# Cross attention's row maxima: one PSUM bank per softmax instead of two banks per group of heads

## The reference, cut to what matters

```
logits_1 = einsum('bhtd,bhsd->bhts', q1, k1) * SCALING
logits_2 = einsum('bhtd,bhsd->bhts', q2, k2) * SCALING
a1 = softmax(logits_1);  a2 = softmax(logits_2)
attn_output = einsum('bhts,bhsd->bhtd', a1 - lam * a2, v)
```

## Time and profile before

| | us |
|---|---|
| median of three runs | 2215.46 |
| the profiled execution | 2225.81 |
| its span, from the first to the last instruction | 2224.0 |
| of it self attention, about | 60 to 800 |
| of it cross attention in steady work, about | 880 to 1700 |
| of it experts and finish, about | 1780 to 2224 |
| VectorE busy over the span | 1303.0 (59%) |
| TensorE matmuls busy over the span | 1711.4 (77%) |

### The profile page before, as it was taken

The page is one execution under the profiler, slowest core; times in us unless marked ns, Lnnn a source line. Parts: engine busy times, 40 slices in busy tenths (PEclk is TensorE's granted clock), DMA queues, the critical chain, the costliest instruction groups (busy, mean ns, idle before and its releaser), DMA issues. The chain is left out here.

```text
span 2224.0 us, 46491 instructions
## 1 busy us (share of the span) xinstructions
PE 1711.4 (77%) x14688; PEld 1214.7 (55%) x14688; DVE 1303.0 (59%) x3032; ACT 1075.7 (48%) x1670; POOL 1236.8 (56%) x1287
## 2 busy tenths in 40 slices
PE   1489999999999845888888888888886359999900
PEld 1356666666666523555555555555553248888800
DVE  2366767676676624777777777777776212222258
ACT  0266666666666523666666666656655112222200
POOL 1566767676676311166666666666665725555423
PEclk9699999999999976988999999989989579999955
DMA  5566666767677426654554545555550035555445
GB/s 197 125 138 158 153 163 147 171 149 171 158 153 168 100 72 106 124 109 98 106 102 101 101 101 102 99 96 103 99 87 25 14 99 124 129 127 126 96 128 179
DMA packets 288971, 267.15 MB, mean 120 GB/s; under 512 B 78962, under 2 KB 273364, under 8 KB 278640
## 3 DMA queue, kind: packets, MB, share of 16 engines
q1 hardware_dynamic: 257648, 244.57, 48.6%
q0 software_dynamic: 22528, 13.03, 3.9%
q10 hardware_dynamic: 8704, 8.39, 1.1%
HBM read 170.57 MB, written 94.30 MB: 119 GB/s over the span
## 5 line engine op out<-in xcount | busy, mean ns | idle before, releaser
L1592 POOL DMA_INDIRECT slot_table<-cross_tok_i,cross_slot_i x384 | 382.6, 996 | 144.6 <-issue 109.3
L598 DVE TENSOR_REDUCE self_nmax<-self_p_mx 128x2 f32<-128x512 f32 x512 | 329.4, 687 | 214.2 <-PE self_p_mx L340 213.8
L1423 DVE TENSOR_REDUCE cross_nmax<-cross_p_mx 128x8 f32<-128x960 f32 x256 | 295.0, 1152 | 210.8 <-PE cross_p_mx L1053 160.0
L510 ACT ACTIVATE self_probs<-self_p_sc 128x1024 f32<-128x1024 f32 x256 | 261.3, 1021 | 95.2 <-PE self_p_sc L328 93.0
L1279 ACT ACTIVATE cross_probs<-cross_p_sc 120x1024 f32<-120x1024 f32 x256 | 261.3, 1021 | 86.0 <-PE cross_p_sc L1037 55.4
L340 PE MATMUL self_p_mx<-self_k_stack,self_q_stack 96*128 96x256 bf16 x1024 | 160.5, 278 | 64.5 <-DMA self_k_stack<-self_k_parts 61.3
L1069 PE MATMUL cross_p_pv<-cross_probs,cross_v_aug 120*32 120x256 f32 x2048 | 176.8, 418 | 9.9 <-ACT cross_probs L1279 6.1
L1053 PE MATMUL cross_p_mx<-cross_k_stack,cross_q_stack 48*128 48x120 bf16 x2048 | 104.5, 225 | 100.4 <-DVE cross_nmax L1423 63.5
L328 PE MATMUL self_p_sc<-self_q_stack,self_k_stack 99*128 99x256 bf16 x1024 | 157.3, 276 | 13.3 <-ACT self_probs L510 12.8
L1956 POOL DMA_INDIRECT expert_sums<-ffn_ye,ffn_idx_add x64 | 92.5, 1445 | 122.0 <-DMA expert_sums<-ffn_ye,ffn_idx_add 53.4
L1037 PE MATMUL cross_p_sc<-cross_q_stack,cross_k_stack 51*128 51x256 bf16 x1024 | 105.8, 287 | 56.5 <-ACT cross_probs L1279 46.7
(11 more groups left out here) (180 smaller groups left out, 3767.6 us busy)
## 6 DMA issues: line engine op xcount, KB each, us to landing
self_q_stack<-self_q_parts SPq DMA_DIRECT2D x64, 256.0 KB, 5.9
cross_q_stack<-cross_q_parts SPq DMA_DIRECT2D x128, 128.0 KB
ffn_w<-in_ffn_w SPq DMA_DIRECT2D x64, 256.0 KB
self_q_parts<-self_parts SPq DMA_DIRECT2D x32, 384.0 KB, 2.8
self_k_parts<-self_parts SPq DMA_DIRECT2D x32, 384.0 KB, 3.8
self_k_stack<-self_k_parts SPq DMA_DIRECT2D x32, 384.0 KB, 8.0
cross_q_parts<-cross_parts SPq DMA_DIRECT2D x64, 192.0 KB
expert_sums<-zero_rows SPq DMA_DIRECT2D x8, 1024.0 KB, 10.2
```

The lines of the kernel that those rows point to most:

```text
L510: act.activation(probs[:, g % 4, :], p_sc[:, :, :].rearrange("p b n -> p (b n)"), ACT.Exp, scale=SCALE).then_inc(s_exp, 1)
L598: dve.tensor_reduce(nmax[:, M.slot, :, m], p_mx[:, m % 2, :].rearrange("p (c k) -> p c k", c=TC), AX_X, ALU.max, negate=True).then_inc(s_r ...
L1423: dve.tensor_reduce(nmax[:, M.slot, :, :, 2 * m:2 * m + 2].rearrange("p c e h -> p e h c"), p_mx[:, :, 0:4 * KEYS].rearrange("p e (x k) -> ...
L1592: pool.indirect_dma_start(out=route[:, :], out_offset=bass.IndirectOffsetOnAxis(ap=slot_i[:, Q.slot, tc, k:k + 1], axis=0), in_=tok_i[:, Q ...
```

## The change

Each group of row maxima is cut into its two softmaxes. TensorE issues the four matmuls of e = 0 and then the four of e = 1, instead of alternating. Before each four it waits until that bank has been reduced in the group before, and after each four it raises `s_mx`. VectorE waits for each bank and reduces it with an instruction of its own (128 x 480 elements to 4 maxima a partition), and each raises `s_red`. So the counts of both semaphores double, to two a group; the one other wait on `s_red`, ahead of the split of the maxima into bf16 parts, counts double too. No memory is added and nothing else is moved.

```diff
-                if m or past(M.n, 1):
-                    pe.wait_ge(s_red, NGR * M.n + m)
-                for hh in range(2):
-                    h = 2 * m + hh
-                    for c in range(TC):
-                        for e in range(E):
+                for e in range(E):
+                    if m or past(M.n, 1):
+                        pe.wait_ge(s_red, E * (NGR * M.n + m) - (E - 1) + e)
+                    for hh in range(2):
+                        h = 2 * m + hh
+                        for c in range(TC):
                             r, q_at = e * HALF, h * T + c * P
                             mm = pe.matmul(p_mx[:, e, (2 * hh + c) * KEYS:(2 * hh + c + 1) * KEYS],
                                            q_stack[r:r + RK, M.slot, q_at:q_at + P],
                                            k_stack[r:r + RK, M.slot, h * KEYS:(h + 1) * KEYS], start=True, stop=True)
-                mm.then_inc(s_mx, 1)
+                    mm.then_inc(s_mx, 1)
...
             def reduce(M, m):
-                dve.wait_ge(s_mx, NGR * M.n + m + 1)
-                if m == 0 and past(M.n, 3):
-                    dve.wait_ge(s_nm, 3 * (M.n - 2))
-                dve.tensor_reduce(nmax[:, M.slot, :, :, 2 * m:2 * m + 2].rearrange("p c e h -> p e h c"),
-                                  p_mx[:, :, 0:4 * KEYS].rearrange("p e (x k) -> p e x k", k=KEYS), AX_X,
-                                  ALU.max, negate=True).then_inc(s_red, 1)
+                for e in range(E):
+                    dve.wait_ge(s_mx, E * (NGR * M.n + m) + e + 1)
+                    if m == 0 and e == 0 and past(M.n, 3):
+                        dve.wait_ge(s_nm, 3 * (M.n - 2))
+                    dve.tensor_reduce(nmax[:, M.slot, :, e, 2 * m:2 * m + 2].rearrange("p c h -> p h c"),
+                                      p_mx[:, e, 0:4 * KEYS].rearrange("p (h c k) -> p h c k", c=TC, k=KEYS), AX_X,
+                                      ALU.max, negate=True).then_inc(s_red, 1)
...
-                    dve.wait_ge(s_red, NGR * (M.n + 1))
+                    dve.wait_ge(s_red, E * NGR * (M.n + 1))
```

## The result

The changed kernel takes 2223.6 us (median of 8 runs), the kernel before took 2215.9 beside it (8 runs): a ratio of 1.0034 [1.0020, 1.0048], so 7.7 us slower. Forecast were 2233 and a range of 2210 to 2256: the sign was right and the size was twice too large. The profiled execution took 2223.86 us, with a span of 2222.1.

What follows compares the result with a forecast made beforehand. Bound: a loop through several engines, with VectorE and TensorE leading in turn. VectorE's 0.30 plus TensorE's 0.35, less 0.04, gave 0.61 us a turn, +18 us over 31 turns: 2215.5 to 2233.5, predicted 2233, range 2210 to 2256.

Steps and rivals of the forecast that it cites:

- VectorE, +0.08 a group, 0.30 a turn: Two reductions of 480 take 1.24 us against 1.152 for one; on the path at m=0 to 3, 0.30 a turn.
- TensorE, +0.15 at m=5 and m=7, 0.35 a turn: Products in softmax order start more slowly, +0.15 us a group on the path at m=5 and m=7; 0.35 with the clock.
- seven steps of which only the one at the seam is free: Eight TensorE products: six of seven steps between starts cost 0.051 us each, 0.31 between first and last start.
- if eight products still take 0.38: Named sign of error: TensorE's eight products of a group lasting 0.38 us as before, where 0.52 was expected.
- m=7 as the way to m=0: TensorE's path runs from L1341 over scores, m=7 and value products to m=0, so m=7's +0.15 us counts.
- the landing 1.96 us behind the modelled end: Before m=0, VectorE's wait was read as products landing later than modelled: 1204.07 against a modelled end of 1202.11.
- The waits added: One more wait on TensorE and one on VectorE; VectorE's costs nothing, TensorE's no more than VectorE's 0.08 us already counted.
- The stretch in which VectorE leads: From m=0 to the end of m=3 VectorE works almost without a gap, so its added time there lengthens the turn.
- Early bank at m=0: Rival: first bank landing at least 0.5 us earlier ends VectorE's reductions sooner at m=0; 2207 to 2211 us, chance 0.13.
- No change: Rival: TensorE's extra 0.15 and half of VectorE's fall into waits; 2216 to 2220 us, chance 0.17.
- The clock: Rival: longer product trains shift TensorE's granted clock either way; 2266 us, or 2205 to 2215; chance 0.12.
- Weight loads laid bare: Rival: each TensorE product runs behind its weight load, +0.97 us a group at m=5 and m=7; 2285 us, chance 0.03.

Runs made afterwards that it cites:

- E1: Kernel before with only VectorE's reduction split in two per group, products in the old order and one signal for both banks: 2219.3 us, 1.0024.
- E8: Kernel before, unchanged, run again for a second profile: 2214.0 us.
- E7: Kernel before with each VectorE reduction cut into four of 240 elements, one signal a group: 2282.4 us, 1.0313.
- E14: Changed kernel with the router's two MAX8 and slots moved behind the reduction of m=4 of the next step: 2171.1 us, 0.9810 of the kernel before.
- E2: Kernel before with only TensorE's order changed, four products of e=0 then four of e=1, waits and signals kept: 2214.7 us, 1.0003.
- E5: Kernel before with VectorE's reduction split only for m=0 to 3: 2216.6 us, 1.0020.
- E10: Kernel before with VectorE's reduction split for every m except m=2: 2214.5 us, 1.0003.
- E11: Kernel before with the router's two MAX8 and slots moved behind the reduction of m=4 of the next step: 2168.7 us, 0.9802.
- E4: Changed kernel with TensorE also waiting for the first softmax's products before issuing the second's: 2303.4 us, 1.0414 of the kernel before.
- E9: Kernel before with VectorE's reduction split only for m=2: 2272.3 us, 1.0265.
- E13: Kernel before with VectorE's reduction split only for m=2 and m=5: 2260.5 us, 1.0205.

## Why the prediction was right in sign and wrong in size

*VectorE, +0.08 a group, 0.30 a turn.* The size of the term was right: 1.22 a pair, 1.24 forecast. E1, which holds this term alone, cost 6.0 us, 9 forecast. Where it lands was only partly right. That its 0.30 a turn comes so near the measured total is luck: 0.09 + 0.32 + 0.06 less the 0.18 that 4>5 and 5>6 give back is 0.29, and the forecast knew neither the step at m=2 nor what is given back. m=0 is not on the path: in E8 the L1443 behind it starts at 1230.59 (above) and ends at 1231.88, just behind GpSimd's L1637, which runs to 1231.72, and takes 1.29 where it takes 0.29 elsewhere. What its reduction adds is lost in that.

```profile
1230.08 1.64 POOL L1637 TENSOR_TENSOR cross_parts<-cross_qk_rest,cross_parts 128x752 bf16<-128x752 f32 x1
```

The distance 0>1 is 4.21 to 4.24 in every kernel of the table but the first profile. m=1 pays 0.09, m=3 0.06, and m=2 pays 0.32, four times its reduction. The price at m=2 has a step in it (E7), and two thirds of the 0.33 sit in the end of L1444 (0.08 + 0.14), the last 0.1 behind the MAX8. GpSimd's chain behind the statistics keeps its own pace. In the change and in E8, the two mask sums together and then the first alone:

```profile
1188.31 0.19 POOL L1655 TENSOR_TENSOR cross_shift<-cross_neg_mean,cross_rstd 128x2 f32<-128x2 f32 x1
1188.46 0.68 POOL L1662 TENSOR_TENSOR cross_mask_sum<-cross_mask_sum,cross_mask 128x64 bf16<-128x64 bf16 x2
...
1188.46 0.30 POOL L1662 TENSOR_TENSOR cross_mask_sum<-cross_mask_sum,cross_mask 128x64 bf16<-128x64 bf16 x1
```

```profile
1238.98 0.20 POOL L1654 TENSOR_TENSOR cross_shift<-cross_neg_mean,cross_rstd 128x2 f32<-128x2 f32 x1
1239.13 0.78 POOL L1661 TENSOR_TENSOR cross_mask_sum<-cross_mask_sum,cross_mask 128x64 bf16<-128x64 bf16 x2
...
1239.13 0.39 POOL L1661 TENSOR_TENSOR cross_mask_sum<-cross_mask_sum,cross_mask 128x64 bf16<-128x64 bf16 x1
```

The mask sums start 2.01 after the statistics in both (1188.46 - 1186.45, 1239.13 - 1237.12). L1443 used to start 0.06 ahead of the first, and took its own 0.29, while GpSimd's took 0.39. Its successor starts 0.03 behind it: now GpSimd's takes 0.30, and L1444 takes 0.42 and ends 0.15 after it (1188.91 against 1188.76). The end stays there when the start moves: in E7 it is again 0.15 after (1203.33 against 1203.18). At m=0 L1443 ends 0.16 after GpSimd's, with a length of 1.29 in E8 and of 0.73 to 0.76 in E7. Single turns of one program agree as well. In E14, 4 of 25 turns in steady work have L1444 start up to 0.02 ahead of the mask sum; it takes 0.29 in them and 2>3 is 2.25 or 2.26. In the 21 others 2>3 is 2.42 to 2.50. So which of the two starts first decides, and this makes the 0.14. What holds the slots behind the MAX8 for the last 0.1 stays open.

The Trainium skill, "SBUF — State Buffer", section "SBUF: two separate sides", says that a VectorE instruction with two inputs in SBUF and a GpSimd instruction that reads SBUF share a pair of ports, which the one that starts first holds to its end. L1443 reads two such inputs, and the trace agrees: in E8 at m=2 GpSimd's, second to start, ends 0.16 after L1443 (1239.52 against 1239.36), and in the change L1444, second to start, ends 0.15 after GpSimd's.

*TensorE, +0.15 at m=5 and m=7, 0.35 a turn.* This is the step that failed. "With the softmaxes one after the other, seven steps of which only the one at the seam is free" took the pace of a single row group in the self stage for the pace of two row groups issued in sequence. Eight products take 0.39, a train of four 0.38, and E2 has 1.0003. The 11 us of this term never came. I had named that as the sign of an error ("if eight products still take 0.38"). The step was also wrong in reading m=7 as the way to m=0: the landing 1.96 us behind the modelled end was in one execution only.

*The waits added.* Nearly right: TensorE's second wait shows as 0.18 in the row above. VectorE's was put at nothing; with the other signals it may be what adds the 0.1 at 2>3 by which the change exceeds E1. The stretch in which VectorE leads, m=1 to m=3, did hold (E5, E10, E11).

*Not foreseen:* 4>5 and 5>6 give back 0.18 a turn, since VectorE waits there for products and the products come no later.

*The rivals.* Early bank at m=0: no idle time there in E8, so there is nothing to gain. No change: refuted by 1.0034 and 1.0042, whose intervals begin at 1.0020 and 1.0025; that rival's own range ended at +4.6 us, and 1.0025 is +5.5. The clock: 0.90 against 0.90 in E8, so not in the change, but it multiplied E4 and E11. Weight loads laid bare: eight products with their eight loads in 0.39 exclude it. The rule of the Trainium skill that the prediction cites beside it ("TensorE: Matmul & The Clock Gate", section "The mechanism") isn't borne out here: in E4 products of one row group start 0.05 apart with loads of 0.09 each.

## What to carry to other kernels

Price an added wait or a split where the engine that issues it leads, and look there for work of another engine that keeps its own pace: here a shift of 0.08 us cost 0.22 because it let the neighbour start first. Don't price an order of issue on TensorE as serial while row groups differ: here eight products over two row groups took 0.39 in either order. When one such stretch bounds the turn, moving unrelated work out of it to a place where the engine waits is worth more than reshaping the handover: here 45 us against a change that cost 8.

## What the runs showed that I had not expected

- Two profiles of the same kernel put the idle time in different places (7>0 4.79 and 3.66). A wait with no plausible releaser is worth a second profile before a step of the sum rests on it.
- VectorE stalled 6.6 to 9.6 us at the back edge of its loop, six times each in E7, E9 and E13; elsewhere this gap is mostly 0.32, and 0.42 in the change. Between two back edges these programs have 344, 275 and 278 of its instructions, waits included; programs of 272, 284, 293, 296 and 321 had no stall. The size of the body alone doesn't sort them, and the cause stays open. An edit of a single instruction on VectorE can so cost 50 us for a reason of its own.
- Less idle time in front of TensorE is paid twice, in the pause and in the clock (E11: 0.82 of 2.0 us a turn is the stretch that lost the work); more idle time costs twice as well (E4).
